# Four block transposes on VectorE in place of one transpose and four ScalarE copies

## The chip, the core and the metric

The kernel runs on one core of a Trainium2 chip. The metric is the device time of one execution in microseconds (us). In the profile the engines are PE (TensorE's matrix multiplications), PEld (its weight loads), DVE (VectorE), ACT (ScalarE), POOL (GpSimd) and SP (SyncE, which issues most DMAs). L756 is line 756 of the kernel.

## The reference, cut to what matters

A layer of cross attention by autocorrelation, followed by a feed-forward network with simulated quantisation, over 128 samples of 128 positions and 256 features (16 heads of 16). For every sample and head the correlation of query and key gives four best lags; their softmax weights mix four rolled copies of the values.

```python
corr = irfft(rfft(Q) * conj(rfft(K)), n=Lv)
top_vals, top_idx = top_k(corr, k_top)          # k_top = 4
w = softmax(top_vals, axis=-1)
for i in range(k_top):
    gather_idx = (t[None, None, :] - top_idx[..., i]) % Dh
    rolled = take_along_axis(V, gather_idx[..., None], axis=2)
    out = out + w[..., i, None] * rolled
...
x = x + xattn(layernorm(x), ctx_1024, ctx_1024, ...)
x = x + ffn(layernorm(x), ...)
```

Since the lag only counts modulo 16, the mixing of one head is a circulant matrix, and that of 128 features a block-diagonal 128x128 matrix. The kernel builds these matrices and multiplies the values by them on TensorE.

## The kernel before

Two samples form a pair; there are 64 (`PAIRS`). The attention runs as a software pipeline written out by hand: each engine has its own list of operations, step by step, and semaphores connect the lists. Each engine works its list strictly in order, so a wait holds up everything behind it on that engine.

TensorE's step t projects keys and values of pair t (`project_k`, `project_v`), projects the attention's output of pair t-4 (`project_out`, L539), projects queries (`project_q`, L477), multiplies the values of pair t-3 by their mixing matrices (`attend`, L527), transforms keys and queries (`dft_k`, `dft_q`, L489 and L501) and transforms the product of pair t-1 back (`inverse`, L556).

VectorE's step t does, in this order: weighting, sums and spreading of the softmax weights of pair t-4 (`weigh_hot` to `spread_weights`, L1215), the four largest correlations of pair t-3 (`top_values`, four MAX8 at L1291, which wait for `inverse`), the transposition of the weights of pair t-4 (`turn_weights`, L1222), the spectrum products of pair t-2 (`products`, L1230 and L1231), the places of the maxima, `one_hot` (L1179), `magnitude` (L1274, which waits for ScalarE's `normalize2`, L762), `residual` (L1238), statistics, and in 22 of the steps one operation that prepares the scales of the feed-forward weights (`weights`, L1104 to L1119).

From `products` the way back to TensorE goes through GpSimd (`add_terms`, L998), ScalarE (`high_cs`, at the shared copy line L686), GpSimd (`low_cs`, L1002, behind `low_ct`, L1010) and then `inverse`.

The mixing weights: `spread_weights` writes `wmask`, 128 partitions by 128 columns, which are four groups (feature half, sample) of 32 columns. `turn_weights` transposes it, which VectorE does within blocks of 32x32, into the compact buffer `blocks`. ScalarE's `spread_blocks` (L756) then copies `blocks`, 32 partitions at a time, into the four diagonal blocks of `mt` (128 partitions, four matrices of 128 columns; cleared once at the start by GpSimd, semaphore `mt_zero`). `attend` reads `mt`. ScalarE's step begins with `spread_blocks`, followed by `take_k` (L686), `take_v` (L730), `normalize2` (L762), `high_ct` and `high_cs` (L686), `exponent`, `take_q_scaled` (L718) and more. The last five pairs are written out one by one, behind the steps, and their turns stand among the other operations of the drain.

Of the kernel before, what the change touches and what calls it, by code (L numbers as in the profile page):

```python
# [6 lines left out]
ACT = mybir.ActivationFunctionType  # L7
# [88 lines left out]
def xattn_ffn_kernel(nc, x, x_turned, ctx_turned, wq, wk, wv, wo, w_in, b_in, w_out, b_out, table, inv_table, out, x1_dram, h_dram):  # L96
# [8 lines left out]
    PAIRS = B // 2  # L105
# [8 lines left out]
    with ExitStack() as ctx:  # L114
# [3 lines left out]
        def sem(name):  # L118
            return ctx.enter_context(nc.semaphore(name))
# [46 lines left out]
        def cut(n, words, shape):  # L166
            a = at[0]
            at[0] += n * words
            assert at[0] <= ARENA
            return [arena[:, a + k * words:a + (k + 1) * words].rearrange(shape[0], **shape[1]) for k in range(n)]  # L170
# [6 lines left out]
        mt = cut(1, 512, FOUR)[0]  # L177
# [11 lines left out]
        SMALL = ("p (g k) -> p g k", dict(g=4))  # L189
# [5 lines left out]
        ssum = cut(1, 4, SMALL)[0]  # L195
        wmix = cut(1, 64, SMALL)[0]
        wmask = cut(1, 128, ("p (g j r) -> p g j r", dict(g=4, j=2)))[0]
        blocks = cut(1, 128, SMALL)[0]
        st1 = cut(1, 12, PAIR)[0]
        st2 = cut(1, 12, PAIR)[0]  # L200
        BOTH = ("p (w b d) -> p w b d", dict(w=2, b=2))
# [39 lines left out]

        names = """const_in direct_in w_in_loaded w_out_in b_in_in b_out_in w_in_scaled ln1_stats
            ln2_stats v_done q_done vt_out q_out terms_done sums_done inv_done sc_top hd_done
            top_done shift_done exp_done mt_out ot_done ot_out ot_low sum_high cs_ready ct_high
            ct_ready w_high w_split y_done x1_done xn1_done xmax_part x_chain ln_chain sc_chain
            xm_ready xmax_all x_scale y_half x1_half xn1_last hot_done ssum_done mul_done rsum_done wsum_done ot_high
            xi_done xhi_done xlo_done b_mm b_gelu b_max hmax_part hmax_all h_scale c_hq c_hi_act
# [4 lines left out]
        S = {n: sem("s_" + n) for n in names}  # L252
# [12 lines left out]
        def wait(eng, s, n):  # L265

            if isinstance(n, int) and n <= 0:
                return
            eng.wait_ge(s, n)

        def upto(n):

            return min(n, PAIRS)

        def active(t, lagged):

            return 0 <= t - lagged < PAIRS
# [155 lines left out]
        def _(pe):  # L433
# [84 lines left out]

            def attend(p, taken=None):

                pe.wait_ge(S["mt_out"], p + 1)
                pe.wait_ge(S["vt_out"], p + 1)
                wait(pe, S["ot_out"], p)
                wait(pe, S["vt_out"], upto(p + 4) if taken is None else taken)
                for c in range(DC):
                    for b in range(2):
                        last = nc.tensor.matmul(four(7)[:, c, b, :], vt[:, p, c, b, :], mt[:, c, b, :], start=True, stop=True)  # L527
                last.then_inc(S["ot_done"], 1)
# [155 lines left out]
        def _(act):  # L684
# [3 lines left out]
            def load_w(n, w):  # L688
                nc.scalar.dma_start(w_attn_raw[:, n, :, :], w.rearrange("(c p) n -> p c n", p=P)).then_inc(s_w_in[n], 16)
# [5 lines left out]
            def high_w(n):  # L695
                if n == 0:
                    act.wait_ge(S["w_centred"], 1)
                else:
                    act.wait_ge(s_w_in[n], 16)
                nc.scalar.activation(w16[:, 0, n], w_attn_raw[:, n], ACT.Copy, scale=W_UP).then_inc(S["w_high"], 1)  # L700

            def exponent(p):
                act.wait_ge(S["shift_done"], p + 1)
                wait(act, S["mul_done"], p - 1)
                wait(act, S["ssum_done"], p - 1)
                nc.scalar.activation(ex[p % 2], shift, ACT.Exp, scale=1.0 / CORR_UP).then_inc(S["exp_done"], 1)

            def take_k(p):
                act.wait_ge(S["kp_done"], p + 1)
                wait(act, S["k_done"], p)  # L710
                copy(kf.rearrange("p b e -> p (b e)"), bank[1][:, :], "kf_out")

            def take_q_scaled(p):
                act.wait_ge(S["qp_done"], p + 1)
                act.wait_ge(S["scales_done"], p + 1)
                wait(act, S["q_done"], p)
                for b in range(2):
                    last = nc.scalar.activation(qf[:, b, :], pair(1)[:, b, :], ACT.Copy, scale=rs[(p + AHEAD) % 2][:, 1, b, :])  # L718
                last.then_inc(S["qf_out"], 1)

            def high_cs(p):
                act.wait_ge(S["sums_done"], p + 1)
                wait(act, S["inv_done"], p)
                copy(cs16[:, 0], csum, "sum_high")

            def take_v(p):
                if p == PAIRS - 8:
                    act.wait_ge(s_win, 16)
                act.wait_ge(S["v_done"], p + 1)
                nc.scalar.activation(xnt[:, p].rearrange("p b d -> p (b d)"), bank[7][:, :], ACT.Copy, scale=1.0 / W_UP).then_inc(S["vt_out"], 1)  # L730

            def high_ct(p):
                act.wait_ge(s_t_in, p * 16 + 16)
                wait(act, S["v_done"], p)
                wait(act, S["kp_done"], p)
                copy(ct16[:, 0], cturn, "ct_high")

            def high_xt(p):
                act.wait_ge(s_xt_in, p * 16 + 16)
                wait(act, S["qp_done"], p)  # L740
                copy(xt16[:, 0], xturn, "xt_high")
# [4 lines left out]
                nc.scalar.activation(qs[:, 0:2, :].rearrange("p r e -> p (r e)"), bank[4][:, :], ACT.Copy, scale=Q_DOWN)  # L746
                nc.scalar.activation(qs[:, 2, :], bank[4][:, 0:D], ACT.Copy, scale=turn).then_inc(S["q_out"], 1)

            def spread_blocks(p):
                if p == 0:  # L750
                    act.wait_ge(S["mt_zero"], 1)
                act.wait_ge(S["bt_done"], p + 1)
                wait(act, S["ot_done"], p)
                for i in range(4):
                    part = slice(32 * i, 32 * i + 32)
                    last = nc.scalar.activation(mt.rearrange("p c b l -> p (c b) l")[part, :, part], blocks[part], ACT.Copy)  # L756
                last.then_inc(S["mt_out"], 1)

            def normalize2(p):
                act.wait_ge(S["scales_done"], p + AHEAD + 1)  # L760
                for b in range(1 if p == PAIRS - 1 else 2):
                    last = nc.scalar.activation(xnt[:, p, b, :], x1[p % 2][:, b, :], ACT.Identity, bias=nm[p % 2][:, b, :], scale=rs[p % 2][:, 0, b, :])  # L762
                last.then_inc(S["xn1_done"], 1)

            def high_ot(p):
                act.wait_ge(S["ot_done"], p + 1)
                wait(act, S["y_done"], p - 1)
                copy(ot16[p % 2][:, 0].rearrange("p c b l -> p (c b l)"), bank[7][:, :], "ot_high")

            def take_ot(p):  # L770
                act.wait_ge(S["ot_high"], p + 1)
                wait(act, S["ot_low"], p - 1)
                copy(ot32[p % 2].rearrange("p c b l -> p (c b l)"), bank[7][:, :], "ot_out")
# [35 lines left out]
            high_w(3)  # L809

            def step(t):
                if active(t, 4):
                    spread_blocks(t - 4)
                if active(t, 1):
                    take_k(t - 1)
                    take_v(t - 1)
                if active(t, 6):
                    normalize2(t - 6)
                if active(t, 0):
                    high_ct(t)  # L820
                    if t == 0:
                        high_w(1)
                if active(t, 2):
                    high_cs(t - 2)
                if active(t, 3):
                    exponent(t - 3)
                if active(t, 1):
                    take_q_scaled(t - 1)
                if active(t, 4):
                    high_ot(t - 4)  # L830
                if active(t, 0):
                    high_xt(t)
                if active(t, 4):
                    take_ot(t - 4)
                if active(t, 1):
                    take_q(t - 1)
                if t == 0:
                    high_w(0)
                if t == 0:
                    load_w(2, wo)  # L840
                if t == 1:
                    high_w(2)
                weights(t)
# [10 lines left out]
            take_v(PAIRS - 2)  # L854
            take_q(PAIRS - 2)
            take_k(PAIRS - 1)
            spread_blocks(PAIRS - 5)
            exponent(PAIRS - 3)
            take_q_scaled(PAIRS - 1)
            high_ot(PAIRS - 5)  # L860
            high_cs(PAIRS - 2)
            take_ot(PAIRS - 5)
            take_q(PAIRS - 1)
            spread_blocks(PAIRS - 4)
            high_ot(PAIRS - 4)
            high_cs(PAIRS - 1)
            take_ot(PAIRS - 4)
            exponent(PAIRS - 2)
            spread_blocks(PAIRS - 3)
            take_v(PAIRS - 1)  # L870
            normalize2(PAIRS - 6)
            high_ot(PAIRS - 3)
            exponent(PAIRS - 1)
            take_ot(PAIRS - 3)
            spread_blocks(PAIRS - 2)
            normalize2(PAIRS - 5)
            high_ot(PAIRS - 2)
            take_ot(PAIRS - 2)
            spread_blocks(PAIRS - 1)
            normalize2(PAIRS - 4)  # L880
            high_ot(PAIRS - 1)
            take_ot(PAIRS - 1)
# [216 lines left out]
        def _(dve):  # L1099
            V = nc.vector  # L1100
# [117 lines left out]
            def turn_weights(p):  # L1218

                dve.wait_ge(S["w2_done"], p + 1)  # L1220
                wait(dve, S["mt_out"], p)
                V.transpose(blocks.rearrange("p g k -> p (g k)"), wmask.rearrange("p g j r -> p (g j r)")).then_inc(S["bt_done"], 1)  # L1222

            def products(p):

# [370 lines left out]
```

## Time and profile before

| | us |
|---|---|
| median of 3 runs (1065.46 to 1065.85) | 1065.5 |
| span of the profiled execution | 1064.2 |
| attention loop, TensorE busy without a gap (34 to 560) | 526.0 |
| fill ahead of it (0 to 34) | 34.0 |
| drain of the last pairs (560 to 592) | 32.0 |
| feed-forward network (592 to the end) | 472 |

Over the whole span PE is busy 1047.4 us (98%), DVE 965.1 (91%), ACT 939.9 (88%), POOL 505.0 (47%). The shares are averages over stages with different limits, so each stage is read by itself. Operations on one engine overlap a little at their ends, so that the start of the next one, not the sum of durations, tells what an operation costs its engine.

### The profile page before, as it was taken

The numbers are of one execution on the slowest core, as the hardware profiler recorded it, in microseconds if no ns is written. First come the engines' busy times: TensorE is split into PE (matmuls) and PEld (weight loads), VectorE is DVE, ScalarE is ACT, GpSimd is POOL, SyncE is SP. The second block draws the span as 40 slices with busy tenths as digits, with TensorE's granted clock in tenths as the row PEclk, the third lists the DMA queues.
The fourth block names the chain that finished last, engine by engine and source line by source line (L and its number), as shares of the span: only waits on it lengthen the run. The fifth ranks groups of instructions, "written<-read, shape, count | busy, mean of one in ns | idle before, by whom it ended". The sixth has DMA issues, their size and how long they took to land.

```text
span 1064.2 us, 28999 instructions
## 1 busy us (share of the span) xinstructions
PE 1047.4 (98%) x9358; PEld 778.0 (73%) x9358; DVE 965.1 (91%) x2768; ACT 939.9 (88%) x1697; POOL 505.0 (47%) x674
## 2 busy tenths in 40 slices
PE   8999999999999999999998899999999999999998
PEld 6788888888888888888887444444444888888887
DVE  4789999999988888888889999999997999999998
ACT  5888888899999998888888688888888999999996
POOL 5788888888888888888887400000001000000000
PEclk9999999999999999999999999999999999999999
DMA  5454444334445443444431498999999999999995
GB/s 178 130 150 145 121 121 120 121 120 120 121 120 140 121 120 120 121 120 120 120 111 41 132 325 301 300 305 316 309 300 342 356 347 363 355 354 355 346 364 195
DMA packets 141665, 222.59 MB, mean 209 GB/s; under 512 B 72432, under 2 KB 92272, under 8 KB 137456
## 3 DMA queue, kind: packets, MB, share of 16 engines
q1 hardware_dynamic: 140464, 220.12, 62.8%
q8 instruction: 61, 1.00, 0.4%
q10 hardware_dynamic: 1088, 1.05, 0.3%
q14 instruction: 52, 0.43, 0.1%
HBM read 121.00 MB, written 83.89 MB: 193 GB/s over the span
## 4 chain that ended last, share of the span: by engine, by line
PE 94%; ACT 2%; DVE 2%; issue 1%; DMA 1%; POOL 0%; ACTq 0%; DVEq 0%; POOLq 0%
PE sums L666 21%; PE bank L635 10%; PE sums L635 10%; PE sums L464 8%; PE sums L477 8%; PE bank L515 8%; PE sums L539 7%; PE sums L489 6%; PE bank L527 5%; PE bank L501 5%; PE bank L556 5%; PE sums L672 1%; DMA store_x<-in_L_xattn_wv 1%; ACT arena L756 0%; ACT arena L686 0%
## 5 line engine op out<-in xcount | busy, mean ns | idle before, releaser
L666 PE MATMUL sums<-wout,arena 128*128 128x256 f16 x2048 | 229.8, 273 | 1.2 <-DVE arena L1521 1.2
L666 PEld LDWEIGHTS sums<-wout,arena 128*128 128x128 f16 x2048 | 196.9, 98 | 32.5 <-DVE arena L1514 7.3
L1521 DVE SCALAR_TENSOR_TENSOR arena<-arena,wout_rel 128x512 f16<-128x512 int16 x256 | 180.3, 746 | 2.0 <-ACT arena L935 0.9
L756 ACT ACTIVATE arena<-arena 32x128 f32<-32x128 f32 x256 | 78.6, 307 | 47.8 <-DVE arena L1222 45.5
L635 PE MATMUL sums<-arena,win 128*128 128x512 f16 x512 | 115.9, 379 | 1.0 <-DVE arena L1466 0.9
L635 PE MATMUL bank<-arena,win 128*128 128x512 f16 x512 | 115.7, 379 | 0.0
L686 ACT ACTIVATE arena<-arena 128x512 f16<-128x512 f32 x192 | 112.9, 617 | 1.6 <-POOL arena L998 1.1
L1485 DVE TENSOR_REDUCE hmax_all<-arena 128x1 f32<-128x1024 f32 x96 | 111.3, 1211 | 2.9 <-ACT arena L892 2.9
L935 ACT ACTIVATE arena<-arena,wout_rel 128x512 f16<-128x512 int16 x159 | 106.2, 706 | 0.0
L892 ACT ACTIVATE arena<-sums,b_in_sb,z_scale 128x512 f32<-128x512 f32 x128 | 97.4, 778 | 9.8 <-PE sums L635 4.9
L1088 POOL CAST store_x<-one 128x1 bf16<-128x1 f32 x1 | 0.2, 189 | 220.0 <-DVE one L1503 220.0
L928 ACT ACTIVATE arena<-arena,one 128x1536 int16<-128x1536 f32 x63 | 99.2, 1575 | 4.5 <-DVE arena L1521 3.0
L1010 POOL TENSOR_TENSOR arena<-arena 128x512 f16<-128x512 f32 x64 | 74.2, 1159 | 54.8 <-ACT arena L686 54.8
L1291 DVE MAX8 arena<-bank 128x8 f32<-128x128 f32 x256 | 57.1, 286 | 46.9 <-PE bank L556 46.8
L477 PE MATMUL sums<-store_x,arena 128*128 128x256 f16 x768 | 94.3, 273 | 1.0 <-ACT arena L686 0.5
L515 PE MATMUL bank<-arena,store_x 128*128 128x256 f16 x768 | 94.3, 273 | 1.0 <-ACT arena L686 0.6
L635 PEld LDWEIGHTS sums<-arena,win 128*128 128x128 f16 x512 | 50.0, 98 | 61.9 <-issue 1.4
L464 PE MATMUL sums<-store_x,arena 128*128 128x256 f16 x768 | 95.0, 273 | 0.0
L635 PEld LDWEIGHTS bank<-arena,win 128*128 128x128 f16 x512 | 50.1, 98 | 60.4
L539 PE MATMUL sums<-store_x,arena 128*128 128x256 f16 x762 | 93.7, 273 | 0.4 <-POOL arena L1006 0.4
L998 POOL TENSOR_TENSOR arena<-arena 128x512 f32<-128x512 f32 x64 | 81.4, 1272 | 3.5 <-DVE arena L1231 3.4
L477 PEld LDWEIGHTS sums<-store_x,arena 128*128 128x128 f16 x768 | 74.9, 98 | 10.4 <-issue 0.8
(141 smaller groups left out, 2303.7 us busy)
## 6 DMA issues: line engine op xcount, KB each, us to landing
hidden_scratch<-arena SPq DMA_DIRECT2D x32, 1536.0 KB, 5.5
arena<-hidden_scratch SPq DMA_DIRECT2D x64, 768.0 KB, 6.7
arena<-in_ctx_turned SPq DMA_DIRECT2D x64, 256.0 KB, 2.6
arena<-in_x_turned SPq DMA_DIRECT2D x64, 256.0 KB, 2.9
arena<-in_x SPq DMA_DIRECT2D x64, 256.0 KB, 3.7
x_scratch<-arena SPq DMA_DIRECT2D x64, 256.0 KB, 3.4
arena<-x_scratch SPq DMA_DIRECT2D x32, 512.0 KB, 6.0
out<-arena SPq DMA_DIRECT2D x31, 512.0 KB, 4.2
```

Of the source, the lines that this page charges most:

```text
L464: last = nc.tensor.matmul(bank[1][:, b * D:(b + 1) * D], ct16[:, i, c, b * P:(b + 1) * P], w16[:, j, 3, c, :], start=c == 0 and k == 0, st ...
L477: last = nc.tensor.matmul(bank[1][:, b * D:(b + 1) * D], xt16[:, i, c, b * P:(b + 1) * P], w16[:, j, 0, c, :], start=c == 0 and k == 0, st ...
L515: last = nc.tensor.matmul(bank[7][:, e * D:(e + 1) * D], w16[:, j, 1, c, e * P:(e + 1) * P], ct16[:, i, c, :], start=c == 0 and k == 0, st ...
L539: last = nc.tensor.matmul(pair(7)[:, 1, :] if p == PAIRS - 1 and b == 1 else pair(0)[:, b, :], ot16[p % 2][:, i, c, b, :], w16[:, j, 2, c, :],
L635: last = nc.tensor.matmul(bank[f][:, :].rearrange("p (n t) -> p n t", n=4), win16[:, f, c, :], xt[q % 3][:, s, :, c, :], start=s == 0 and ...
L666: last = nc.tensor.matmul(bank[m * 2 + k // 2][:, k % 2 * D:(k % 2 + 1) * D], gbuf[:, s, f, k * P:(k + 1) * P], wout16[:, f, :], start=f = ...
L686: nc.scalar.activation(dst, src, ACT.Copy).then_inc(S[done], 1)
L892: nc.scalar.activation(dst, bank[b][:, :], ACT.Gelu, bias=b_in_sb[:, f:f + 1], scale=z_scale[:, f:f + 1]).then_inc(S[done], 1)
L928: nc.scalar.activation(hq[:, a:b, :].rearrange("p f t -> p (f t)"), src, ACT.Copy, scale=h_up).then_inc(S["c_hq"], 1)
L935: nc.scalar.activation(gbuf[:, 0, f, :], hq[:, f, :], ACT.Copy, scale=wout_rel[:, f:f + 1]).then_inc(S["c_hi_act"], 1)
L1485: V.tensor_reduce(hmax[:, bass.ds(q, 1), k], halls[m][:, 2 * k:2 * k + 2, :], AX_XY, ALU.max, apply_absolute_value=True).then_inc(S["b_max ...
L1521: V.scalar_tensor_tensor(gbuf[:, 1, f, :], hq[:, f, :], wout_rel[:, f:f + 1], gbuf[:, 0, f, :], ALU.mult, ALU.subtract).then_inc(S["c_lo"], 1)
```

## The change

The compact buffer and ScalarE's copies go. VectorE transposes `wmask` in four operations, each of 32 partitions by 128 columns, straight into the diagonal blocks of `mt`. The waits that the copies carried (`mt_zero` for the first pair, `ot_done` for the pair before) move to VectorE, and `attend` waits for `bt_done`, the transposes' semaphore.

```diff
@@ sizes
         wmask = cut(1, 128, ("p (g j r) -> p g j r", dict(g=4, j=2)))[0]
-        blocks = cut(1, 128, SMALL)[0]
@@ TensorE
             def attend(p, taken=None):
-                pe.wait_ge(S["mt_out"], p + 1)
+                pe.wait_ge(S["bt_done"], p + 1)
@@ ScalarE
-            def spread_blocks(p):
-                if p == 0:
-                    act.wait_ge(S["mt_zero"], 1)
-                act.wait_ge(S["bt_done"], p + 1)
-                wait(act, S["ot_done"], p)
-                for i in range(4):
-                    part = slice(32 * i, 32 * i + 32)
-                    last = nc.scalar.activation(mt.rearrange("p c b l -> p (c b) l")[part, :, part], blocks[part], ACT.Copy)
-                last.then_inc(S["mt_out"], 1)
...
             def step(t):
-                if active(t, 4):
-                    spread_blocks(t - 4)
...
@@ VectorE
             def turn_weights(p):
                 dve.wait_ge(S["w2_done"], p + 1)
-                wait(dve, S["mt_out"], p)
-                V.transpose(blocks.rearrange("p g k -> p (g k)"), wmask.rearrange("p g j r -> p (g j r)")).then_inc(S["bt_done"], 1)
+                if p == 0:
+                    dve.wait_ge(S["mt_zero"], 1)
+                wait(dve, S["ot_done"], p)
+                for i in range(4):
+                    part = slice(32 * i, 32 * i + 32)
+                    last = V.transpose(mt.rearrange("p c b l -> p (c b) l")[part, :, part], wmask.rearrange("p g j r -> p g (j r)")[part])
+                last.then_inc(S["bt_done"], 1)
```

The five calls of `spread_blocks` for the last pairs go as well.

## Rows read from the trace of the kernel before

**Rows 1.** Busy time by stretch: stretch, length, busy us of each engine, clock, DMA.

```profile
34.00:560.00 526.00, 526.00 (x5678) 432.65 (x5678) 473.45 (x1971) 465.49 (x1085) 452.58 (x589) 1.00 0.42 124
560.00:592.00 32.00, 27.19 (x268) 20.52 (x264) 28.57 (x113) 25.35 (x60) 21.88 (x38) 1.00 0.14 51
```

**Rows 2.** Lines L756 and L1222: min/median/max ns; its wait's end; who waited (us, times).

```profile
L756 ACT ACTIVATE arena<-arena x256: 292/308/311, 31.4 to 582.0; 32x128 f32<-32x128 f32 x128
  DVE arena L1222: 45.5, 59
  PE bank L527: 2.0, 3
...
L1222 DVE STREAM_TRANSPOSE arena<-arena x64: 293/294/311, 31.0 to 580.5; 128x128 f32<-128x128 f32 x64
```

**Rows 3.** Timeline, VectorE, one step: start, us, line, count, [idle before <- releaser].

```profile
305.24 0.89 DVE L1291 MAX8 arena<-bank 128x8 f32<-128x128 f32 x4 [0.85 <-PE bank L556]
306.05 0.29 DVE L1222 STREAM_TRANSPOSE arena<-arena 128x128 f32<-128x128 f32 x1
306.27 0.65 DVE L1230 TENSOR_TENSOR arena<-arena,sums 128x512 f32<-128x512 f32 x1
306.84 0.68 DVE L1231 TENSOR_TENSOR arena<-arena,sums 128x512 f32<-128x512 f32 x1
...
309.37 0.41 DVE L1179 TENSOR_TENSOR sums<-cst,sums 128x256 f32<-128x256 f32 x1
309.90 0.69 DVE L1274 TENSOR_REDUCE xmax<-store_x 128x1 f32<-128x512 f32 x1
...
314.13 0.89 DVE L1291 MAX8 arena<-bank 128x8 f32<-128x128 f32 x4 [0.85 <-PE bank L556]
```

**Rows 4.** Timeline, ScalarE, the copies of one step and what follows them.

```profile
306.38 1.26 ACT L756 ACTIVATE arena<-arena 32x128 f32<-32x128 f32 x4 [0.55 <-DVE arena L1222]
307.66 0.60 ACT L686 ACTIVATE arena<-sums 128x512 f32<-128x512 f32 x1
308.16 0.59 ACT L730 ACTIVATE store_x<-bank 128x512 f32<-128x512 f32 x1
```

**Rows 5.** Line L1104 (first of its two groups), and VectorE's timeline around weight operations.

```profile
L1104 DVE TENSOR_REDUCE win_max<-store_x x8: 401/402/404, 89.6 to 151.8; 128x1 f32<-128x256 f32 x8
...
154.05 0.89 DVE L1291 MAX8 arena<-bank 128x8 f32<-128x128 f32 x4 [0.52 <-PE bank L556]
...
178.49 0.88 DVE L1119 TENSOR_SCALAR win_up<-win_up 128x8 f32<-128x8 f32 x1
...
180.73 0.89 DVE L1291 MAX8 arena<-bank 128x8 f32<-128x128 f32 x4
```

**Rows 6.** Timeline, GpSimd and TensorE, the way from `products` to `inverse`.

```profile
308.17 1.28 POOL L998 TENSOR_TENSOR arena<-arena 128x512 f32<-128x512 f32 x1
...
310.47 1.16 POOL L1010 TENSOR_TENSOR arena<-arena 128x512 f16<-128x512 f32 x1 [0.85 <-ACT arena L686]
311.58 1.16 POOL L1002 TENSOR_TENSOR arena<-arena 128x512 f16<-128x512 f32 x1
...
304.36 0.84 PE L556 MATMUL bank<-inv,arena 64*128 64x128 f16 x24
```

**Rows 7.** Timeline at the start, ScalarE and TensorE, first pair with copies.

```profile
31.35 1.27 ACT L756 ACTIVATE arena<-arena 32x128 f32<-32x128 f32 x4 [1.01 <-DVE arena L1222]
...
33.38 1.47 PE L477 MATMUL sums<-store_x,arena 128*128 128x256 f16 x12 [0.54 <-ACT arena L686]
```

**Rows 8.** Timeline, VectorE, the drain: operations with idle time before them, and L1274.

```profile
568.57 0.69 DVE L1230 TENSOR_TENSOR arena<-arena,sums 128x512 f32<-128x512 f32 x1 [0.44 <-ACT arena L747]
...
575.02 0.89 DVE L1291 MAX8 arena<-bank 128x8 f32<-128x128 f32 x4 [0.17 <-PE bank L556]
...
581.24 0.69 DVE L1238 SCALAR_TENSOR_TENSOR arena<-sums,arena 128x512 f32<-128x512 f32 x1 [0.44 <-PE sums L539]
...
582.91 1.84 DVE L1274 TENSOR_REDUCE xmax<-store_x 128x1 f32<-128x512 f32 x3
```

More of the change, by code:

```diff
@@ L243, in xattn_ffn_kernel @@
             ln2_stats v_done q_done vt_out q_out terms_done sums_done inv_done sc_top hd_done
-            top_done shift_done exp_done mt_out ot_done ot_out ot_low sum_high cs_ready ct_high
+            top_done shift_done exp_done ot_done ot_out ot_low sum_high cs_ready ct_high
             ct_ready w_high w_split y_done x1_done xn1_done xmax_part x_chain ln_chain sc_chain
@@ L856, in _ @@
             take_k(PAIRS - 1)
-            spread_blocks(PAIRS - 5)
             exponent(PAIRS - 3)
@@ L863, in _ @@
             take_q(PAIRS - 1)
-            spread_blocks(PAIRS - 4)
             high_ot(PAIRS - 4)
@@ L868, in _ @@
             exponent(PAIRS - 2)
-            spread_blocks(PAIRS - 3)
             take_v(PAIRS - 1)
@@ L874, in _ @@
             take_ot(PAIRS - 3)
-            spread_blocks(PAIRS - 2)
             normalize2(PAIRS - 5)
@@ L878, in _ @@
             take_ot(PAIRS - 2)
-            spread_blocks(PAIRS - 1)
             normalize2(PAIRS - 4)
```

## The prediction

> **What bounds the kernel now.** I read the stages first, then the waits around the change, then one step of each engine. In the stage table [rows 1] the reader should look at TensorE (PE): from 34 to 560 us, the attention loop, it is busy 526.00 of 526.00 us at a granted clock of 1.00. Nothing taken from another engine can shorten that stretch; it can only be lengthened. PE has idle time only ahead of it, while the pipeline fills, and in the drain of the last pairs (4.8 of 32 us); the stage behind contains nothing of the change. VectorE (DVE) is busy 473 of the 526 us. The copies that go (L756) stand behind 45.5 us of ScalarE (ACT) idle time, a tempting number, but only 2.0 us of it reach PE, three times, all in the drain [rows 2]. So ACT's relief is worth little, and the question is what VectorE's room bears.
>
> That room is read from one step of the loop [rows 3]. `top_values` (four MAX8) starts at 305.24 and again at 314.13: the step is 8.89 us, PE's own. VectorE waits 0.85 us of it for PE's inverse transform. It also waits before `magnitude` (L1274): the operation in front starts at 309.37 and takes 0.41, its follower could start some 0.08 before that ends, at 309.70, and starts at 309.90, because ACT's `normalize2` ends only then. That wait goes when VectorE gets later and ACT earlier. With 0.06 for the usual overlap at MAX8, VectorE needs 8.89 - 0.85 - 0.20 - 0.06 = 7.78 us for a step, so it has 1.1 us of room.
>
> **What the change removes.** ACT loses four copies, 1.26 us a pair, and the 0.5 us or so that it waits ahead of them [rows 4]. In the loop that buys nothing: PE has no idle time to give back. No DMA, and no step of the SP or GpSimd (POOL) queue, is moved.
>
> **What it adds, for each pair.** One transpose of 128x128 becomes four of 32x128. The columns stay 128 for each, and duration follows columns: 0.29 us now, and ACT's copies of 32x128 take 0.307 to 0.308 at the same count of columns [rows 2, 3]. How close the four can follow one another is not shown for VectorE, since none of its operations here begins off partition 0. Two bounds. From below: the transpose starts at 306.05 and its successor at 306.27, so an overlapped one costs 0.22, three more 0.66. From above: ACT's copies are the only ones that step through the four partition groups, with the very same slices of `mt`. Four of 0.307 need 1.26 [rows 4]: no overlap at all. And `take_k` behind them starts at 307.66, after their end at 307.64, although its input from PE was long there; the next ordinary pair overlaps (0.60 from 307.66, next start 308.16). Stepping to another partition group costs the overlap, for the four and for the operation behind. I take this row: it is the same access on a neighbour engine. VectorE's four then need 4 x 0.294 [rows 2] plus some 0.01 between, 1.22 in all, and `products` starts only after them. **Added: 1.22 - 0.22 = 1.00 us a pair.** Ends: 0.66, and 1.2 if each needs 0.35 (writing in strides is the unseen part). Less than 0.66 would need transposes shorter than their row, for which the unchanged 128 columns give no reason.
>
> Beside that stands the Trainium skill, page "VectorE: DVE Perf Modes", section "Two Vector instructions with no wait between them": a Vector operation whose input or output starts in another group of 32 partitions than the last one's begins only when all earlier ones have finished. By that rule the four and `products` run one by one, as the ACT rows do, which is the 1.00; by the overlap of VectorE's own rows it would be 0.66 and a time of 1066.2. No VectorE row here decides between them.
>
> **The wait that moves.** `turn_weights` now waits itself for `attend` of the pair before (`ot_done`), with all of VectorE's queue behind it: `products` first, and PE's inverse behind that. In the loop VectorE reaches it only after MAX8, whose inverse stands behind that `attend` in PE's queue. So it is fulfilled on arrival and costs 0. In the drain the turns come later by the sum below and the `attend` ahead of them do not, so I take 0 there too; it would cost what it waits, once for each pair.
>
> **The loop's sum.** With 1.00 more, an ordinary step is 8.78 against PE's 8.89: 0.11 spare, no loss. But 22 steps also carry a weight operation (`weights`). The 16 with a maximum (L1104, two groups of 8, the first shown) leave 0.52 idle instead of 0.85 [rows 5], so they need 0.33 more, 9.11: 0.22 too long. Two scalings (L1119) take 0.88, and the two floors (L1109) as much; MAX8 behind the one shown, at 180.73, has no idle time ahead of it. They need 9.6, about 0.7 too long each. Two reciprocals fit. VectorE falls behind by 16 x 0.22 + 4 x 0.71 = 6.4 us. PE does not feel the first part. Going round from MAX8: 0.81 to the transposes, 1.22, `products` 1.25, then POOL's queue with L998 1.28, L1010 1.16 and L1002 1.16, then PE's L556 0.84 and some 0.15 for handing over, 7.9 us [rows 3, 6] against 8.89. PE therefore tolerates a lag of some 1.0, and **5.4 us** reach it, between about 130 and 280 us. Afterwards some 30 ordinary steps recover the lag at 0.11 each. A second way to the same order: 473 + 58 x 1.0 = 531 us of VectorE work do not fit into 526 [rows 1].
>
> **Start.** At 33.38 PE waits 0.54 for `take_k`, which stands in ACT's queue behind the first copies (31.35, 1.27) [rows 7]. With them gone PE could be up to 0.7 earlier, but the products of the same step are 1.0 later and reach PE through POOL and ACT in that step. Between -0.7 and 0 I take **-0.3**.
>
> **Drain.** The three waits of PE for L756 [rows 2] go, yet VectorE is late next. From 568 us on it has four turns to do and 4.0 us more work. Its idle time takes up 0.44, 0.17 and 0.44, each with 0.07 of overlap that a wait had cost: 1.3 in all. From the three `magnitude` at 582.91 on it shows no idle time up to the last residual, which the rest of the kernel follows [rows 8]. So **+2.7**, in place of the 2.0 that ACT's removal seems to promise.
>
> **Sum.** 5.4 + 2.7 - 0.3 = +7.8 us on the profiled span of 1064.2. The median of the runs is 1065.5, 1.3 above the span, and I add the same to it: 1073.3 us. A measurement of this kernel can tell about 0.2%, 2.1 us, from no change.
>
> **Rivals.**
> - *Overlapped transposes* (0.66 more): an ordinary step is 8.44, one with a maximum 8.77, and the four long ones run 0.36 over, which the tolerated lag takes up. Loop 0, drain 4 x 0.66 - 1.3 = +1.3, start -0.6: 1066.2. For it: every VectorE row overlaps. Against: ACT's copies.
> - *VectorE bounds every step.* From 1.11 added on, the ordinary step is over 8.89 too. At 1.2 each of 58 steps needs 0.2 more than in the forecast, less the 0.11 spare in 36 ordinary ones: +7.6, and the drain 4 x 0.2 more: 1081.7. For it: 0.11 is a thin margin, worked out from overlaps. This is the slower end.
> - *The drain gives back* what PE waits for L756, with transposes well below their row: -2.0 and -0.6, 1062.9. For it: the three waits are in the chain that ends the stage. Against: VectorE's rows from 582.91 on have no room, and added work there must be under 0.35 a turn.
> - *The change does not do what it says*: ACT is released but waits for PE in place of VectorE, so nothing of its 1.8 us a step is used. That is already so in the loop; at the start it makes 0.3 of difference and is inside the range.
>
> **How the numbers follow.** Forecast 0.70: between 1069 (some 0.87 added) and 1077 (some 1.1 added). Overlapped 0.14, VectorE in every step 0.11, drain gives back 0.05. The likeliest case gives 1073.3; the range 1068.5 to 1082 takes in the forecast's bounds and most of the slow rival, and leaves out under 2 in 10. Faster by over 0.2%: 0.05; within: 0.14; slower: 0.81.
>
> **What the profile after would show.** Four transposes of about 0.29 in 1.2 us, and `products` beginning after them; if they take 0.95 in all, the overlap rival holds. MAX8's idle time near 0.1 in ordinary steps and none from about 90 to 280 us; PE idle some 5 us within 130 to 280, and not at all from 300 to 555. ACT's wait for L1222 gone, its idle time now ahead of `take_k` or `take_v`, on PE. In the drain, PE's waits for the last two `attend` on VectorE. The forecast is wrong if PE stays full up to 280 us, or if it also idles from 300 to 555 us.

## The result, and the profile after

The changed kernel takes 1075.48 us (median of 4 runs, 1075.36 to 1076.93); the kernel before, run beside it, 1065.66. The ratio is 1.0095, with a 95% interval of 1.0082 to 1.0107: 9.8 us slower. The profiled span is 1073.7 us against 1064.2.

The page's first part (busy time, share of the span, instructions of each engine):

```profile
PE 1052.0 (98%) x9358; PEld 776.4 (72%) x9358; DVE 1020.2 (95%) x2960; ACT 869.8 (81%) x1441; POOL 507.4 (47%) x674
```

ScalarE lost 70 us of work and VectorE gained 55, and the time followed VectorE. The stage table (stretch, length, busy us of each engine, clock, DMA), for the loop and then for the part of it that holds no weight operations:

```profile
34.00:560.00 526.00, 522.50 (x5593) 424.28 (x5591) 517.59 (x2119) 396.87 (x841) 448.91 (x583) 1.00 0.42 123
...
290.00:560.00 270.00, 269.35 (x2902) 220.89 (x2900) 266.74 (x1095) 208.26 (x441) 234.72 (x305) 1.00 0.42 121
```

Against [rows 1], where TensorE was busy 526.00 of 526.00 us, it now has holes, and VectorE is busy 98% of the loop. All but 0.65 us of the holes lie ahead of 290 us. The holes are smaller than the loss, since a matmul's end is modelled and short waits vanish in it. Starts don't have that fault. TensorE's inverse transforms of the same two pairs, near the first and the last step of the loop, after:

```profile
37.30 0.84 PE L555 MATMUL bank<-inv,arena 64*128 64x128 f16 x24
...
560.07 0.84 PE L555 MATMUL bank<-inv,arena 64*128 64x128 f16 x24
```

and before:

```profile
37.55 0.84 PE L556 MATMUL bank<-inv,arena 64*128 64x128 f16 x24
...
553.37 0.84 PE L556 MATMUL bank<-inv,arena 64*128 64x128 f16 x24
```

At 37 us the changed kernel is 0.25 ahead, at 560 us 6.70 behind: the loop lost 6.95. From 293 to 560 us the difference stays at 6.70. At the statistic that ends the attention on VectorE, after and before,

```profile
601.72 0.22 DVE L1432 TENSOR_REDUCE one<-xmax 128x1 f32<-128x65 f32 x1
...
591.93 0.22 DVE L1445 TENSOR_REDUCE one<-xmax 128x1 f32<-128x65 f32 x1
```

it is 9.79, so the drain lost 3.1. The rest of the kernel gave back 0.3 in the two profiled executions. That is not the change's: 0.25 of it is VectorE's first quantisation (L1451 at 603.30), which took 0.75 us here and 1.00 before, and 1.00 again in e7_other_floors, a later run with the same transposes.

One ordinary step of VectorE after, the counterpart of [rows 3]:

```profile
312.46 0.89 DVE L1278 MAX8 arena<-bank 128x8 f32<-128x128 f32 x4
313.26 1.23 DVE L1208 STREAM_TRANSPOSE arena<-arena 32x128 f32<-32x128 f32 x4
314.52 0.69 DVE L1217 TENSOR_TENSOR arena<-arena,sums 128x512 f32<-128x512 f32 x1
...
317.67 0.41 DVE L1161 TENSOR_TENSOR sums<-cst,sums 128x256 f32<-128x256 f32 x1
317.99 0.68 DVE L1261 TENSOR_REDUCE xmax<-store_x 128x1 f32<-128x512 f32 x1
...
321.28 0.89 DVE L1278 MAX8 arena<-bank 128x8 f32<-128x128 f32 x4
```

The four transposes take 1.23 us, and `products` (L1217) starts 1.26 after their start, against 0.22 before: 1.04 added a pair. From MAX8 to MAX8 it is 8.82 us, with no idle time. Two steps with more work in them, one with a maximum (91.81 to 100.95) and one with a floor (155.82 to 165.52):

```profile
91.81 0.89 DVE L1278 MAX8 arena<-bank 128x8 f32<-128x128 f32 x4
99.31 0.40 DVE L1086 TENSOR_REDUCE win_max<-store_x 128x1 f32<-128x256 f32 x1
100.95 0.89 DVE L1278 MAX8 arena<-bank 128x8 f32<-128x128 f32 x4
...
155.82 0.89 DVE L1278 MAX8 arena<-bank 128x8 f32<-128x128 f32 x4
163.33 0.95 DVE L1091 TENSOR_SCALAR win_max<-win_max 128x8 f32<-128x8 f32 x1
165.52 0.89 DVE L1278 MAX8 arena<-bank 128x8 f32<-128x128 f32 x4
```

They last 9.14 and 9.70 us, longer than TensorE's 8.89.

Where does VectorE's lag reach TensorE? This is the only wait of TensorE in the loop that the table of waits lists (engine, tile and line that waited, released by, us in total, times, longest):

```profile
PE bank L500 <- ACT arena L717: 3.1, 6, 0.6
```

L500 is `dft_q`, and L717 is ScalarE's `take_q_scaled`. The step that follows the floor shows how it comes about (rows of four engines, in order of time):

```profile
168.19 0.68 DVE L1218 TENSOR_TENSOR arena<-arena,sums 128x512 f32<-128x512 f32 x1
...
168.95 1.27 POOL L980 TENSOR_TENSOR arena<-arena 128x512 f32<-128x512 f32 x1 [1.55 <-DVE arena L1218]
...
170.10 1.08 PE L488 MATMUL sums<-arena,cst 128*64 128x256 f32 x8
...
170.25 0.63 ACT L685 ACTIVATE arena<-arena 128x512 f16<-128x512 f32 x1 [1.21 <-POOL arena L980]
170.89 0.82 ACT L717 ACTIVATE arena<-sums,arena 128x256 f32<-128x256 f32 x2
...
171.46 1.16 POOL L984 TENSOR_TENSOR arena<-arena 128x512 f16<-128x512 f32 x1
...
171.77 1.08 PE L500 MATMUL bank<-arena,cst 128*64 128x256 f32 x8 [0.58 <-ACT arena L717]
172.78 0.84 PE L555 MATMUL bank<-inv,arena 64*128 64x128 f16 x24
```

The late `products` hold up GpSimd's `add_terms` (L980), that holds up ScalarE's `high_cs` (L685), and `take_q_scaled` stands behind `high_cs` in ScalarE's list. The queries' transform, which needs nothing of those products, is late because its input waits in a queue. In undisturbed steps `dft_q` starts 0.91 or 0.92 us after `dft_k` (L488); here it is 1.67, and nearly all of the loop's 6.95 us lie in that gap and in the overlap lost behind it. GpSimd's `low_cs` (L984), on the direct way to `inverse`, is nearly as late; the part on the prediction compares the two ways.

### The profile page after: what moved, and what is told of

It reads as the page before. It is cut to its first block and busy times, and to the rows that moved or that the text cites. A ratio compares the mean times of both kernels' runs of the same rounds, so it can differ in the third digit from the quotient of the medians.

```text
span 1073.7 us, 28872 instructions
## 1 busy us (share of the span) xinstructions
PE 1052.0 (98%) x9358; PEld 776.4 (72%) x9358; DVE 1020.2 (95%) x2960; ACT 869.8 (81%) x1441; POOL 507.4 (47%) x674
## 5 line engine op out<-in xcount | busy, mean ns | idle before, releaser
L685 ACT ACTIVATE arena<-arena 128x512 f16<-128x512 f32 x192 | 118.5, 625 | 22.9 <-POOL arena L980 21.8
L980 POOL TENSOR_TENSOR arena<-arena 128x512 f32<-128x512 f32 x64 | 81.4, 1273 | 52.3 <-DVE arena L1218 52.2
L538 PE MATMUL sums<-store_x,arena 128*128 128x256 f16 x762 | 94.8, 275 | 1.0 <-POOL arena L988 1.0
L685 ACT ACTIVATE arena<-sums 128x512 f32<-128x512 f32 x66 | 39.3, 596 | 60.0 <-PE sums L463 60.0
L514 PEld LDWEIGHTS bank<-arena,store_x 128*128 128x128 f16 x768 | 75.0, 98 | 11.2 <-issue 1.9
L538 PEld LDWEIGHTS sums<-store_x,arena 128*128 128x128 f16 x762 | 74.9, 98 | 10.3 <-POOL arena L988 1.2
L476 PEld LDWEIGHTS sums<-store_x,arena 128*128 128x128 f16 x768 | 75.0, 98 | 9.6 <-DVE store_x L1114 0.8
```

Source lines behind the costliest of these rows:

```text
L476: last = nc.tensor.matmul(bank[1][:, b * D:(b + 1) * D], xt16[:, i, c, b * P:(b + 1) * P], w16[:, j, 0, c, :], start=c == 0 and k == 0, st ...
L514: last = nc.tensor.matmul(bank[7][:, e * D:(e + 1) * D], w16[:, j, 1, c, e * P:(e + 1) * P], ct16[:, i, c, :], start=c == 0 and k == 0, st ...
L538: last = nc.tensor.matmul(pair(7)[:, 1, :] if p == PAIRS - 1 and b == 1 else pair(0)[:, b, :], ot16[p % 2][:, i, c, b, :], w16[:, j, 2, c, :],
L685: nc.scalar.activation(dst, src, ACT.Copy).then_inc(S[done], 1)
```

## The experiments

**1. What a step between partition groups costs.** Theory: the transposes lose their overlap because each begins in another group of 32 partitions than the last. Rival: a transpose of 32x128 written in strides is slow by itself. The first kernel has all four transposes on partitions 0 to 31 (it leaves out the mixing of three groups), the second on the groups 0, 0, 2, 2 (it leaves out the mixing of two).

```diff
@@ e1_same_group
-  last = V.transpose(mt...[part, :, part], wmask...[part])
+  last = V.transpose(mt...[0:32, :, part], wmask...[0:32])
@@ e2_two_groups
+  group = slice(64 * (i // 2), 64 * (i // 2) + 32)
+  last = V.transpose(mt...[group, :, part], wmask...[group])
```

> The changed kernel, but all four transposes read and write partitions 0 to 31 (same columns of mt, same strides; the mixing of three partition groups is left out). Theory: stepping from one group of 32 partitions to another takes the overlap away. Then four transposes in about 0.95 us instead of 1.23, products 0.22 after the start of the last, MAX8 waiting again 0.4 us an ordinary step, no loss in the loop, and 1065.5 to 1067 us (1066.2). Rival: strided writing or transposing itself forbids overlap: 1.23 us as before, no idle time at MAX8, 1075.5 us.

> The changed kernel, but the four transposes use partition groups 0, 0, 2, 2 (the mixing of two groups is left out): two steps between groups (one inside, one back to products) instead of four. Theory: the price is paid per step, so about half of the 0.38 us comes back: four in 1.1 us or a little under, an ordinary VectorE step of 8.6, one with a maximum of 8.95, loop loss about 2, drain +2.2: 1069 to 1070.5. Rival (strides or the operation itself): 1075.5.

Measured: 1065.56 us (ratio 0.9999, 0.9989 to 1.0008) and 1067.46 us (1.0017, 1.0007 to 1.0027). VectorE's timeline, one group:

```profile
304.87 0.86 DVE L1208 STREAM_TRANSPOSE arena<-arena 32x128 f32<-32x128 f32 x4
305.66 0.64 DVE L1217 TENSOR_TENSOR arena<-arena,sums 128x512 f32<-128x512 f32 x1
```

and two groups:

```profile
305.57 0.98 DVE L1208 STREAM_TRANSPOSE arena<-arena 32x128 f32<-32x128 f32 x4
306.59 0.69 DVE L1217 TENSOR_TENSOR arena<-arena,sums 128x512 f32<-128x512 f32 x1
```

From the transposes' start to that of `products` it is 0.79 with no change of group, 1.02 with two and 1.26 with four (the return to partition 0 counts): 0.12 us for each change. With one group the same shape, strides and count leave the kernel's time where it was before the change (by TensorE's and VectorE's starts 0.7 us is gained at the start, nothing lost in the loop, 0.5 lost in the drain), and each transpose takes 0.256 instead of 0.302. The theory holds. The second kernel took less than expected: with 0.80 added in place of 1.04 an ordinary step needs 8.57 us, so a long one is soon made up for, and one floor and one scaling took 0.15 us instead of 0.95 (the other two 0.97 and 0.95; experiment 4 tells why), so that the loop lost only 0.3.

**2. The same on ScalarE.** The prediction read the price from ScalarE's copies [rows 4]. The kernel before, with the copies all on partitions 0 to 31 (it leaves out the mixing of three groups):

```diff
-  last = nc.scalar.activation(mt...[part, :, part], blocks[part], ACT.Copy)
+  last = nc.scalar.activation(mt...[0:32, :, part], blocks[0:32], ACT.Copy)
```

> The kernel before, but ScalarE's four copies all read and write partitions 0 to 31 (the mixing of three groups is left out). Theory: ScalarE loses its overlap by stepping between groups as VectorE does, so the four take about 0.9 us instead of 1.26 and take_k overlaps their end; the time stays within 0.3 us of 1065.5 or gains a little in the drain. Rival, copies of this size never overlap: 1.26.

Measured: 1064.61 us, one run, 1.1 below the kernel before and so less than expected; half of that is there at the start, where TensorE's first and third `inverse` lie 14.9 us apart instead of 15.4. ScalarE's timeline:

```profile
305.80 0.91 ACT L756 ACTIVATE arena<-arena 32x128 f32<-32x128 f32 x4 [0.55 <-DVE arena L1222]
306.62 0.57 ACT L686 ACTIVATE arena<-sums 128x512 f32<-128x512 f32 x1
```

0.91 us instead of 1.26, and `take_k` again starts before the copies end. So the rows that the price was read from had the cause which the prediction gave them, and it works on both engines.

**3. Loop and drain apart.** The change for the first 59 pairs alone, and for the last five alone; the other pairs keep the compact buffer and ScalarE's copies (`copied(p)` counts those up to pair p).

```diff
+  def direct(p): return p < PAIRS - 5        # e3_loop_only
+  def direct(p): return p >= PAIRS - 5       # e4_drain_only
   def turn_weights(p):
+      if not direct(p):
+          wait(dve, S["mt_out"], copied(p - 1))
+          V.transpose(blocks..., wmask...).then_inc(S["bt_done"], 1)
+          return
+      ...                                    # four direct transposes
   def spread_blocks(p):
+      if direct(p): return
```

> Direct transposes for the first 59 pairs, the old way (compact buffer and ScalarE copies) for the last five, written out in the drain. Theory: the loop's loss of 6.9 us stays and the drain's 3.1 goes: 1072.2 us. Rival, the drain is where most is lost: 1068 or less.

> The old way for the first 59 pairs, direct transposes for the last five only. Theory: VectorE bounds the drain, +3.1: 1068.6 us. Rival, the drain gives back what TensorE waits for ScalarE's copies there (2.0 us): 1063.5 to 1065.5.

Measured: 1072.41 us (1.0063, 1.0047 to 1.0080), which is 6.6 more than before, and 1068.85 us (1.0029, 1.0018 to 1.0041), 3.1 more. TensorE's waits from 34 to 605 us, the two largest, first of the loop-only kernel:

```profile
PE bank L509 <- ACT arena L729: 3.1, 6, 0.6
PE bank L538 <- ACT arena L769: 2.0, 3, 1.3
```

and of the drain-only one:

```profile
PE bank L538 <- DVE arena L1243: 3.1, 2, 2.0
PE bank L523 <- ACT arena L697: 1.6, 1, 1.6
```

The two losses add up to the whole (6.6 + 3.1 = 9.7), and each stage keeps its own waits: `dft_q` on `take_q_scaled` in the loop, `attend` on VectorE's transposes (L1243) in the drain, in place of the 2.0 us on ScalarE's copies.

**4. Is it the weight operations that overfill the loop?** Theory: only steps with a maximum, floor or scaling are too long. Rival: VectorE bounds every step. First the maxima were cut to 8 of 256 columns (so the scales are incomplete) and floors and scalings written as another operation, then that other operation alone; then floors and scalings were made to read their 8 columns from PSUM (the on-chip memory that TensorE writes its results to) instead of SBUF (the on-chip memory that holds the other tiles), alone and with the short maxima.

```diff
@@ e5_light_weights, e7_other_floors (floors; scalings alike)
-  V.tensor_scalar(top_, top_, TINY, None, ALU.max)
+  V.scalar_tensor_tensor(top_, top_, TINY, top_, ALU.max, ALU.max)
@@ e5_light_weights, e10_psum_light
-  V.tensor_reduce(top_[:, k:k + 1], raw[:, k, :], ...)
+  V.tensor_reduce(top_[:, k:k + 1], raw[:, k, 0:8], ...)
@@ e9_psum_floors, e10_psum_light
+  w_small = bank[2][:, 2 * P + 32:2 * P + 32 + FC]     # PSUM
   # maxima and reciprocals write w_small
-  V.tensor_scalar(top_, top_, TINY, None, ALU.max)
+  V.tensor_scalar(top_, w_small, TINY, None, ALU.max)
```

> The changed kernel with the weight operations of its 22 steps made small: the maxima (L1086) over 8 columns instead of 256 (so the scales of the feed-forward weights are left incomplete), floors and scalings (L1091, L1101) in another operation form that takes no scalar path with GpSimd. Theory: the loop loses only where a step of VectorE exceeds 8.89; an ordinary one needs 8.82, these now some 8.90, so the whole 6.9 us of the loop come back: 1068.5 us, TensorE without idle time from 90 to 560 us. Rival, VectorE or the moved wait holds TensorE in ordinary steps too: 1072 or more.

> The changed kernel, with only the two floors and two scalings in the other operation form, same result. Theory: each takes about 0.16 us instead of 0.95, since it no longer waits for GpSimd's running operation; VectorE's lag falls by 4 x 0.8 = 3.2 us and so does the time: 1072.3 us. Rival, the form makes no difference: 1075.5.

> The changed kernel, same result, but maxima and reciprocals of the weights are written to PSUM, so that floors and scalings (L1091, L1101) read PSUM instead of SBUF. The earlier run with another operation form left them at 0.95 us, ending together with GpSimd's running operation. Theory: what waits for GpSimd is a VectorE operation that reads SBUF through the path it shares with GpSimd; reading PSUM, each takes 0.15 to 0.2 us, VectorE's lag falls by 4 x 0.8 = 3.2 us, and the time to 1072.3 us. Rival, they wait for GpSimd for another reason (writing SBUF): 1075.5.

> As the run before, and the maxima over 8 columns instead of 256 (so the scales of the feed-forward weights are left incomplete). Theory: with both, no step of VectorE needs over 8.9 us and the whole loss of the loop comes back: 1068.7 us, which is the drain's 3.1 alone, and TensorE without idle time from 90 to 560 us. Rival, ordinary steps lose too: 1070 or more.

Measured, in this order: 1071.85 us (1.0057, 1.0040 to 1.0074); 1075.78 (1.0093, 1.0076 to 1.0110); 1072.54 (1.0063, 1.0047 to 1.0078); 1068.81 (1.0028, 1.0017 to 1.0040). The first two missed what was expected and came out close to their rivals' times: their premise, that the other form does not wait for GpSimd, was wrong, and it is as long (0.94 to 1.09 us). So e5_light_weights can't tell the theory from its rival, and e10_psum_light does. The floors by line (min/median/max ns, first and last start), in e7_other_floors:

```profile
L1091 DVE SCALAR_TENSOR_TENSOR win_max<-win_max x1: 950/950/950, 163.5 to 163.5; 128x8 f32<-128x8 f32 x1
```

and in e9_psum_floors:

```profile
L1092 DVE TENSOR_SCALAR win_max<-sums x1: 150/150/150, 163.5 to 163.5; 128x8 f32<-128x8 f32 x1
```

Reading from PSUM, the floor takes 0.15 us, though it still writes SBUF; that gives back 2.9 us. With the maxima short as well, nothing of the loop's loss is left. The stage table of e10_psum_light:

```profile
90.00:290.00 200.00, 200.00 (x2170) 164.48 (x2167) 197.29 (x835) 152.92 (x324) 173.20 (x225) 1.00 0.41 123
290.00:560.00 270.00, 270.00 (x2910) 222.10 (x2910) 266.80 (x1096) 208.65 (x442) 234.24 (x305) 1.00 0.40 121
```

TensorE is full in both stretches although VectorE still does the four transposes of every step, and the time is that of the drain alone (1068.81 against 1068.85 in experiment 3). The rival falls.

Why is the floor long? Its time goes with GpSimd's. Before, the floor runs from 160.70 to 161.58, and GpSimd's operation beside it, L1002, from 160.40 to 161.56. After, GpSimd:

```profile
163.10 1.16 POOL L996 TENSOR_TENSOR arena<-arena 128x512 f16<-128x512 f32 x1 [0.16 <-ACT arena L685]
```

It ends at 164.26, the floor at 164.28. In e1_same_group a floor that starts at 159.87 beside an operation ending at 160.04 takes 0.21; in e2_two_groups it falls between two operations of GpSimd and takes 0.15; in e9_psum_floors it lies inside one (163.23 to 164.39) and takes 0.15 from PSUM.

**5. What ScalarE's relief is worth.** The kernel before without the copies (it leaves out the mixing, and the matrices stay zero; VectorE keeps its one transpose, and `attend` waits for that).

```diff
   def spread_blocks(p):
-      ...
+      return
```

> The kernel before with ScalarE's copies left out and nothing added to VectorE (the attention's mixing is left out, its matrices stay zero): ScalarE's relief by itself. Theory: the loop gives nothing, the start some 0.1 to 0.6 us, the drain less than the 2.0 us of TensorE's waits, since VectorE is next: 1064 to 1065.2 us. Rival, relief is worth all three waits and the start: 1062.9 or less.

Measured: 1064.04 us against 1065.68 (0.9984, 0.9974 to 0.9994): 1.6 us. VectorE's three `magnitude` of the drain, which stood at 582.91 in [rows 8]:

```profile
581.51 1.84 DVE L1268 TENSOR_REDUCE xmax<-store_x 128x1 f32<-128x512 f32 x3
```

They come 1.4 earlier, and the statistic that ends the attention 1.6 (590.31 instead of 591.93). 0.6 of it is there at the drain's first `products` (561.93 instead of 562.53) and is the start's: from TensorE's first `inverse` to its third it is 14.7 us instead of 15.4. The drain gains 1.0, though TensorE had waited 2.0 for the copies.

**6. A kernel that takes the gain without the price.** The kernel before, with `take_k` ahead of the first copies, and with GpSimd making half of the copies for the last two pairs. Everything is computed.

```diff
@@ ScalarE, step(t)
+  if t == 4: take_k(t - 1)
   if active(t, 4): spread_blocks(t - 4)
@@ spread_blocks
-  for i in range(4):
+  for i in range(2 if shared(p) else 4):
@@ GpSimd, last two pairs
+  ...                                        # waits
+  for i in range(2, 4):
+      last = nc.gpsimd.tensor_copy(mt...[part, :, part], blocks[part])
```

> The kernel before, same result, with two things that the runs point to: in step 4 ScalarE does take_k ahead of the first copies (start), and for the last two pairs GpSimd makes two of the four copies beside ScalarE (drain). ScalarE's relief alone, with the copies left out, was worth 0.6 at the start and 0.8 in the drain. Theory: 0.6 of the start and some 0.4 of the drain: 1064.7 us, ratio 0.9990, at the edge of what can be told. Rival, VectorE bounds the drain and GpSimd's copies are slow: 1065.1 to 1065.7.

Measured: 1065.21 against 1065.73 (0.9995, 0.9986 to 1.0004): not to be told from no change, and within the rival's times. The trace separates the two parts. From TensorE's first `inverse` to its third it is 14.9 us instead of 15.4, so the start gives 0.5 of the 0.6 expected. The drain gives nothing: the profiled execution is 1.15 us ahead at 553 us and 1.13 at the statistic that ends the attention. The copies on GpSimd and what TensorE waits for now:

```profile
576.37 0.62 POOL L1029 COPY arena<-arena 32x128 f32<-32x128 f32 x2 [1.20 <-DVE arena L1245]
580.23 0.62 POOL L1029 COPY arena<-arena 32x128 f32<-32x128 f32 x2
```

```profile
PE bank L532 <- POOL arena L1029: 0.8, 1, 0.8
```

A copy takes 0.31 there too, and the wait, 1.3 us before, is still 0.8 and now for GpSimd. For the last pair GpSimd comes to its copies behind other work: they start at 580.23, and the transpose had ended at 579.64. No version measurably faster than the kernel before, with everything computed, was found.

## Why the prediction was right, and where its terms were off

The forecast was 1073.3 us, +7.8; measured was +9.8, within the range. The loop cost 6.95 instead of 5.4, the drain 3.1 instead of 2.7, and the start gave 0.1 instead of 0.3: all three miss in the same direction, so no error hid another one. Step by step:

- **TensorE bounds the loop and can only lose.** Right. With all copies away (e6_no_copies) the kernel gains 1.6 us, at the start and in the drain.
- **1.00 us a pair.** Right in cause, 0.04 low: 1.04. A transpose took 0.302 rather than 0.294 us. The rule of the Trainium skill, page "VectorE: DVE Perf Modes", section "Two Vector instructions with no wait between them", that an operation starting in another group of partitions is held until the earlier ones have finished, agrees with these runs: 0.79, 1.02 and 1.26 us for none, two and four changes.
- **The wait that moves costs 0.** Right: in the loop the transposes start 0.80 after MAX8 (0.81 before), and no transpose of the whole run, the drain's included, has idle time ahead of it.
- **The wait ahead of `magnitude` goes.** Right: L1261 starts 0.32 after the start of its predecessor (317.67 and 317.99); before it was 0.53 [rows 3].
- **The loop, +5.4.** Right in mechanism (e9_psum_floors, e10_psum_light), 6.95 measured. VectorE's excess was put at 6.4. From MAX8 at 82.65 to 286.00 it is 203.35 us, and 22 steps of TensorE, at 8.893 each ((553.37 - 37.55) / 58), are 195.6: 7.7. Of the difference, 16 steps at 9.14 instead of 9.11 make 0.5, four floors and scalings at 0.81 over instead of 0.71 make 0.4 (their wait for GpSimd fell longer), and one idle 0.29 us ahead of L1197 at 220.85, which the profile puts down to no other engine, makes 0.3.
- **The way back to TensorE.** This step failed, though by little. The prediction went from GpSimd's `low_cs` to `inverse` and found a tolerance of 1.0. The way that binds goes through ScalarE's queue to `dft_q`: 6.25 us from MAX8 (165.52) to L500 (171.77), 1.01 to `inverse` and its 0.84 make 8.10, so the tolerance is 0.8. The predicted way was almost level: L984 ended at 172.62, 0.16 ahead of `inverse`, which needs 0.05 where it waits for L984 alone (575.08 to 575.13, in the drain). By itself that way would have taken 8.0 and left 0.9. So `dft_q` is what binds, but taking it off that way, by another order of ScalarE's list, could by these rows give back no more than 0.1 us; it was not run. 7.7 - 0.8 = 6.9 gives the measured loss. TensorE's own starts agree: `inverse` falls behind from 108.45 us on and not from about 130, after three of VectorE's long steps, which make 0.8.
- **Start, -0.3.** About -0.1: of the 0.25 at 37 us, 0.13 was there at 22 us, ahead of any transpose.
- **Drain, +2.7.** 3.1; 4 x 1.04 - 1.3 gives 2.9, and 0.2 stays open.
- **The rivals.** Overlapped transposes: that is what e1_same_group is, 1065.56 against the 1066.2 given. VectorE in every step: excluded by e10_psum_light. The drain gives back: no, e4_drain_only loses 3.1. ScalarE's waits went where the last part of the prediction said:

```profile
ACT arena L685 <- PE sums L463: 55.9, 58, 1.2
ACT store_x L729 <- PE bank L514: 41.4, 58, 0.8
```

- **Signs that failed.** MAX8 was to show 0.1 us idle in late steps and shows none. An operation that follows without a wait starts some 0.08 before its predecessor's end here (at 321.28 MAX8 starts, at 321.37 L1197 in front of it ends), so the 0.07 that a step of 8.82 has to spare shows as lost overlap: from about 390 us on the steps are 8.89 and MAX8 starts 0.27 instead of 0.20 after L1197. And in the drain one `attend` waits for VectorE, not two (in e4_drain_only it is two):

```profile
586.66 1.16 PE L526 MATMUL bank<-arena,store_x 128*128 128x128 f32 x8 [1.95 <-DVE arena L1208]
587.76 2.58 PE L538 MATMUL sums<-store_x,arena 128*128 128x256 f16 x12
590.14 1.64 PE L567 MATMUL sums<-cst,store_x 128*128 128x128 f32 x8
591.61 1.06 PE L526 MATMUL bank<-arena,store_x 128*128 128x128 f32 x8
592.50 1.47 PE L538 MATMUL sums<-store_x,arena 128*128 128x256 f16 x12
```

The last `attend` (591.61) finds its transposes done at 591.20; TensorE itself was late, for the reason told at the end.

## What to carry to other kernels

Price an added operation by the time from its start to the next one's start, on its engine and in its partition group, and add it to the fullest step of that engine, not to the mean one: 1 us fitted into ordinary steps and cost 7 us through the 20 that hold a maximum, a floor or a scaling. Follow a delay through the queues, since the operation that becomes late may need nothing of the delayed data and only stand behind something that does; here that way was 0.1 us longer than the direct one. An engine that is full all through a loop takes nothing from the relief of another one, except in the fill and the drain.

## What the runs showed of the hardware that was not expected

- **A change of the partition group costs both VectorE and ScalarE their overlap.** The forecast took this from ScalarE's rows; the runs that stay in one group show it on both engines. For 32x128 it is about 0.12 us a change on VectorE. On ScalarE four copies take 1.26 us with the changes and 0.91 without.
- **A small VectorE operation with its input in SBUF can last as long as GpSimd's running one.** The floors of 128x8 took 0.88 and 0.95 us beside an operation of GpSimd, until its end; 0.15 between two; 0.15 from PSUM beside one. Reciprocals of the same shape (0.19) were not affected. That VectorE's second read interface to SBUF is shared with GpSimd stands in the Trainium skill, page "VectorE: DVE Perf Modes", section "Two Vector instructions with no wait between them"; which interface the floors used, no run here shows.
- **TensorE's clock fell in the drain.** The stage table of after, around the longest wait of the drain:

```profile
585.00:586.00 1.00, 0.00 (x0) 0.00 (x0) 0.97 (x6) 1.00 (x4) 0.36 (x1) 1.00 0.00 0
586.00:587.00 1.00, 0.34 (x3) 0.34 (x4) 0.92 (x5) 0.54 (x2) 0.79 (x1) 1.00 0.00 0
...
588.00:589.00 1.00, 1.00 (x7) 0.74 (x5) 1.00 (x5) 0.97 (x2) 0.00 (x0) 0.50 0.53 203
589.00:590.00 1.00, 1.00 (x7) 0.69 (x6) 0.87 (x7) 0.09 (x1) 0.68 (x3) 0.50 0.16 59
```

The granted clock is 0.50 (the lower of the two levels, 1.2 of 2.4 GHz) from 588 to 591 us, after TensorE had waited 1.95 us at 584.7, and L538 took 2.58 instead of 1.47 us. Before, it was 1.00 throughout the drain. It was 1.00 there in e4_drain_only too, with waits of 2.0 and 1.6 us and the same loss of 3.1 us. Of the changed kernel's four runs, one has a mean clock of 1.000 over its span and took 1075.36 us; two, the profiled one among them, have 0.998 and took 1075.46 and 1075.50; the fourth has 0.997 and took 1076.93, and what made it longer is not shown. So the clock is not what made the drain longer by 3.1 us, and which wait tips it is not shown.
